# A state-space layer with a mixture of experts: blocks of the scan joined in pairs, and the residual written into PSUM

## What is computed

```python
xz = rms(xn) @ in_proj.T;  x_s, z = split(xz)            # 512 channels each
u = silu(conv4(x_s) + conv_b)                            # causal, 4 taps, per channel
dt_raw, B, C = split(u @ x_proj.T)                       # 16, 16, 16
delta = softplus(dt_raw @ dt_proj.T + dt_b)
h[t] = exp(delta[t] * A) * h[t-1] + (delta[t]*u[t]) * B[t]   # 16 states per channel
y[t] = sum_s h[t, :, s] * C[t, s] + u[t] * D
mamba = (y * silu(z)) @ out_proj.T + xn
ffn = top-2 of 8 experts, w2(silu(w1 xn) * (w3 xn)), weighted by the gate
```

## Time and profile before

| | before |
|---|---|
| median of three runs | 2660.86 us |
| profiled execution: its own time / its span | 2653.93 / 2652.2 us |
| TensorE busy | 2292.8 us, 86% |
| VectorE busy | 2459.2 us, 93% |
| ScalarE busy | 1658.9 us, 63% |
| GpSimd busy | 2031.0 us, 77% |
| mean granted TensorE clock | 0.936 |

### The profile page before, as it was taken

The page is one execution under the profiler, slowest core; times in us unless marked ns, Lnnn a source line. Parts: engine busy times, 40 slices in busy tenths (PEclk is TensorE's granted clock), DMA queues, the critical chain, the costliest instruction groups (busy, mean ns, idle before and its releaser), DMA issues. The chain is left out here.

```text
span 2652.2 us, 47132 instructions
## 1 busy us (share of the span) xinstructions
PE 2292.8 (86%) x14442; PEld 1986.7 (75%) x14442; DVE 2459.2 (93%) x4041; ACT 1658.9 (63%) x4137; POOL 2031.0 (77%) x1607
## 2 busy tenths in 40 slices
PE   3958789899999999998999989999989899998665
PEld 2855578878787887877888877888877787887554
DVE  7679999999999999999999999999999999999997
ACT  3940566666666666666666666666666666666653
POOL 3430678888888888888888888888888888888883
PEclk7858899999999999999999999999999999999776
DMA  7216045565555555555555555555555555542451
GB/s 244 92 40 216 29 124 156 154 176 152 161 151 152 157 160 171 158 157 153 155 160 155 166 163 151 158 156 160 154 162 164 156 152 157 159 113 52 96 100 32
DMA packets 267099, 379.38 MB, mean 143 GB/s; under 512 B 21492, under 2 KB 158324, under 8 KB 266852
## 3 DMA queue, kind: packets, MB, share of 16 engines
q1 hardware_dynamic: 236196, 332.26, 40.2%
q0 software_dynamic: 28480, 43.94, 10.1%
q10 hardware_dynamic: 2176, 0.18, 0.1%
HBM read 332.59 MB, written 52.10 MB: 145 GB/s over the span
## 5 line engine op out<-in xcount | busy, mean ns | idle before, releaser
L475 POOL TENSOR_TENSOR h<-du,bbc 128x512 f32<-128x512 f32 x1024 | 1362.5, 1354 | 505.3 <-PE HT L1305 375.3
L1071 DVE TENSOR_TENSOR_SCAN h<-DA,carry,h 128x256 f32<-128x256 f32 x2048 | 1417.7, 734 | 91.4 <-ACT DA L748 79.0
L748 ACT ACTIVATE DA<-delta,alog 128x256 f32<-128x256 f32 x2048 | 882.6, 468 | 212.2 <-DVE h L1071 200.9
L1305 PE MATMUL HT<-ident,h 128*128 128x128 f32 x4096 | 665.8, 288 | 260.5 <-DVE yT L1082 259.1
L1305 PEld LDWEIGHTS HT<-ident,h 128*128 128x128 f32 x4096 | 496.6, 148 | 416.2 <-issue 375.2
L1082 DVE SCALAR_TENSOR_TENSOR yT<-HT,cT,yT 128x512 f32<-128x512 f32 x960 | 698.5, 728 | 3.1 <-PE HT L1305 3.1
L1354 PE MATMUL G<-xtT,W 128*128 128x128 f32 x2160 | 273.2, 281 | 0.0
L1368 PE MATMUL G<-W,fill 128*128 128x256 f32 x1080 | 271.8, 397 | 0.0
L1361 PE MATMUL G<-xtT,W 128*128 128x128 f32 x2160 | 263.4, 275 | 0.0
L1354 PEld LDWEIGHTS G<-xtT,W 128*128 128x128 f32 x2160 | 261.1, 198 | 0.0
L1361 PEld LDWEIGHTS G<-xtT,W 128*128 128x128 f32 x2160 | 252.2, 192 | 0.0
(11 more groups left out here) (183 smaller groups left out, 2986.6 us busy)
## 6 DMA issues: line engine op xcount, KB each, us to landing
W<-in_w_T_dram SPq DMA_DIRECT2D x405, 512.0 KB, 4.2
bbc<-b_dram SPq DMA_DIRECT2D x256, 256.0 KB, 4.3
xraw<-in_x_dram SPq DMA_DIRECT2D x64, 256.0 KB, 2.7
xn_dram<-W SPq DMA_DIRECT2D x8, 1032.0 KB, 14.0
W<-in_x_dram SPq DMA_DIRECT2D x32, 256.0 KB, 6.7
moe_dram<-fill SPq DMA_DIRECT2D x32, 256.0 KB, 4.0
out_dram<-tmpA SPq DMA_DIRECT2D x32, 256.0 KB, 2.2
out_dram<-moe_dram POOLq DMA_DIRECT2D x32, 256.0 KB, 4.4
```

The lines of the kernel that those rows point to most:

```text
L475: pool.tensor_tensor(h[:, v % RING], du[:, b, 2 * q:2 * q + 2, :], bbc[:, s // 2 % BRING, s % 2, :].unsqueeze(1).to_broadcast([P, 2, T]), ...
L748: i = act.activation(DA[:, v % 2, k, :], delta[:, b, c, :], ACT.Exp, scale=nega[:, c, s:s + 1])
L1071: i = dve.tensor_tensor_scan(h[:, v % RING, k, :], DA[:, v % 2, k, :], h[:, v % RING, k, :], carry[:, b, s, c:c + 1], ALU.mult, ALU.add)
L1305: i = pe.transpose(HT[:, k, c * P:(c + 1) * P], h[:, (2 * s + c // 2) % RING, c % 2, k * P:(k + 1) * P], ident[:, :])
```

## The change

Blocks 2 to 29 are joined in pairs of the same batch row, 512 time steps in all (`LONG = 2` short blocks stay at either end). The number of units stays: a unit of a pair is one chunk (k = 0 to 3) of one state over 512 steps, still 128x512 elements. So `scan` and `make_da` are one instruction of 128x512 instead of two of 128x256, `keep_carry` comes once per four units, and TensorE turns a state's four units once all four are scanned: unit u at step u + 4, added at step u + 6. The ring `h` has three groups of four units in pairs (eight units before), `delta`, `du`, `u2` hold two pairs each, as rows of 512 of which a front writes one half of 256. The front of block n is done in block n - 2 instead of n - 1, and its back in block n + 2 instead of n + 1 (other places for the first and last blocks). Weight slots go from 5 to 3 experts, the ring of B rows from 4 to 3.

The residual is written by ScalarE into PSUM `FA` at step 26 (before: into SBUF at step 17); the output product starts on it (`start=False`) at steps 27 and 28, and ScalarE copies the sum into `res` at step 30. VectorE's add `result` is gone.

```diff
-            def make_da(blk, v):
-                (j, b), (s, q) = blk, divmod(v, 2)
...
-                for k in range(2):
-                    c = 2 * q + k
-                    i = act.activation(DA[:, v % 2, k, :], delta[:, b, c, :], ACT.Exp, scale=nega[:, c, s:s + 1])
...
+                if is_long(n):
+                    i = act.activation(DA[:, g % 2, :], delta_pair[n // 2 % 2][:, k, :], ACT.Exp, scale=nega[:, k, s:s + 1])
...
+                if is_long(n):
+                    i = dve.tensor_tensor_scan(h(g), DA[:, g % 2, :], h(g), carry[:, b, s, k:k + 1], ALU.mult, ALU.add)
...
+                if is_long(n):
+                    pool.tensor_tensor(h(g), du_pair[n // 2 % 2][:, k, :], bbc[:, g // 4 % BRING, :], ALU.mult).then_inc(s_dbu, 1)
...
+                if k == 0:
+                    pe.wait_ge(s_scan, g + (4 if is_long(n) else 2))
...
+            def residual(n):
+
+                act.wait_ge(s_xres, 16 * (n + 1))
+                if n + 5 <= NB:
+                    act.wait_ge(s_sp, 2 * (n + 5))
+                act.wait_ge(s_y, 2 * n + 2)
...
+                    act.activation(FA[:, t, :], xraw[:, t, :], ACT.Identity, bias=at_col(nm, q),
...
+            def result(n):
+                act.wait_ge(s_omm, NT * (n + 1))
+                wait(act, s_mamba, 16 * n)
+                act.wait_ge(s_delta, min(n + 5, NB))
+                act.copy(res, FA[:, :, :]).then_inc(s_res, 1)
...
-                                  start=(c == 0), stop=(c == CH - 1))
+                                  start=False, stop=(c == CH - 1), skip_group_check=True)
```

More of the change, by code:

```diff
@@ L208, in build @@
         NPAR = 16 * 6
[L210 to L230, removed]
@@ new lines, in turned, with tile_start, tiles_at, fills @@
+        def turned(g, after=0):
+            return [u for u in range(max(0, g - after - 8), min(g - after + 1, UNITS)) if turn_at[u] + after == g]
+        def tile_start(i):
+            return 2 * U * (J0 + i // PER) + U * (i % PER // len(XT_UNITS)) + XT_UNITS[i % len(XT_UNITS)]
+        def tiles_at(g, stage):
+            for i in range(NTILES):
+                if tile_start(i) + stage == g:
+                    return i
+            return None
+        def fills(i, ring):
+            return i // ring + 1
@@ L278, in build @@
[L278 to L284 removed]
+        BACK = {"z0": -1, "tanh_z0": 0, "silu_z0": 1, "z1": 2, "tanh_z1": 3, "silu_z1": 4, "y0": 4, "gate_y0": 6, "y1": 5,
+                "gate_y1": 7, "reload": 7, "oacc": 26, "out0": 27, "out1": 28, "result": 30}
+        AT = {(name, n): U * max(n - 2, 0) + at for name, at in FRONT.items() for n in range(1, NB)}
@@ L424, in _ @@
+            for g in range(UNITS):
+                step(g)
+            store_out(NB - 1)
+            sp.wait_ge(s_bst, 16 * NB)
+            sp.wait_ge(s_mamba, 16 * NB)
+            sp.wait_ge(s_add, 16 * NB)
         @block.gpsimd
@@ L569, in _ @@
+            for g in range(UNITS):
+                step(g)
+            add_result(NB - 1)
         @block.scalar
@@ L857, in _ @@
+            for g in range(UNITS):
+                step(g)
+            residual(NB - 1)
+            result(NB - 1)
         @block.vector
@@ L1177, in _, with step @@
-            run(step)
-            last = (JB - 1, 1)
-            for u in range(32 - LAG, 32):
-                add_state(last, u)
+            def step(g):
+                scan(g)
+                tile_a2(g)
+                for u in turned(g, 2):
+                    if state_of(u)[0]:
+                        add_state(u)
+                tile_ha(g)
+                if g == ROUTE:
+                    route()
+                    place()
+                    invert()
+                for q in range(2):
+                    for n in due(f"silu_z{q}", g):
+                        silu_z(n, q)
+                    for n in due(f"gate_y{q}", g):
+                        gate_y(n, q)
+                for q in range(2):
+                    for n in due(f"silu_u{q}", g):
+                        silu_u(n, q)
+                for q in range(2):
+                    for n in due(f"sp{q}", g):
+                        relu_ln(n, q)
@@ L1181, in _, with transpose_x @@
+            for g in range(UNITS):
+                step(g)
+            for g in range(UNITS, UNITS + 4):
+                for u in turned(g, 2):
+                    add_state(u)
             for q in range(2):
-                silu_z(*last, q)
-            for q in range(2):
-                gate_y(*last, q)
-            result(*last)
+                gate_y(NB - 1, q)
         @block.tensor
         def _(pe):
-            def transpose_x(j, b):
-                n = number(j, b)
+            def transpose_x(n):
@@ L1447, in _ @@
+            for g in range(UNITS):
+                step(g)
+            for g in range(UNITS, UNITS + 4):
+                for u in turned(g):
+                    transpose_h(u)
+            for q in range(2):
+                y_mm(NB - 1, q)
             for t in range(NT):
-                out_mm(*last, t)
+                out_mm(NB - 1, t)
 def kernel(**inputs):
```

1005 lines of the change are left out of this document (494 added, 511 removed), and 2 rows, old and new, of the table SLOTS.

## The result

The changed kernel takes 2639.1 us, median of 9 runs (2632.3 to 2645.8), against 2660.9 (9 runs of the kernel before beside them). The ratio is 0.9915, 95% interval 0.9892 to 0.9937, so it is 0.85% faster. The profiled execution has a span of 2636.2 us; before it was 2652.2, so the two traces differ by 16.0 us.

What follows compares the result with a forecast made beforehand. The prediction took a loop of GpSimd's leg, VectorE's handover and TensorE's leg as the bound, not VectorE alone. From 2653.93 us profiled, -56 for blocks and +19 for clock falls gave 2617 us, range 2575 to 2652.

Steps and rivals of the forecast that it cites:

- Scan and decay: VectorE's scan of 512 near 1.27 us, saving 0.12 a unit; ScalarE's decay near 0.68, saving 0.2 us on GpSimd's path.
- The two legs: GpSimd's stretch, VectorE's handover and TensorE's stretch form the block's loop: 24.2, 2.06 and 48.8 us, together 75.1; chance 0.50.
- Today the loss falls where GpSimd is awaited anyway: Kernel before, step 23: TensorE's half-clock loss of 1.7 us was said to fall where GpSimd is awaited.
- TensorE's leg: From TensorE's turning to the end of the next H1: 50.49 us falls by 1.7 to 48.8 as waits for VectorE shrink.
- Turning behind it waits 0.5 + 1.6 = 2.1 us.: At step 32 VectorE arrives 1.7 us early, the GpSimd term does not, so TensorE's turning waits 2.1 us.
- The clock, +19 us: TensorE falls to half clock after its new wait in four blocks of ten, 1.7 us each, over 28 blocks.
- Ends: I put them at nothing, within 8 us.: Short blocks, the crowded front of block 2 and the tail were together taken to change nothing, within 8 us.
- VectorE alone: Rival: VectorE sets the pace, so all 4.4 us a block come through, 124 us, giving 2530 us; chance 0.12.
- Clock in every block: Rival: TensorE's clock falls in every block, taking back 48 of the 56 us, giving 2646 us; chance 0.17.
- GpSimd's operations longer: Rival: large operations and driving terms lengthen GpSimd's path by 3.5 us a block, +42 us, giving 2696 us; chance 0.10.
- Front and back two blocks away: Rival: doing front and back two blocks away causes an unseen wait of 1 us a block, 2645 us; chance 0.11.
- Residual and copy at nothing: ScalarE's residual and copy, steps 26 to 30, put at nothing; if uncovered, 1.2 + 0.6 us a block.

Runs made afterwards that it cites:

- before_wait_after: Kernel before, without pairs, with GpSimd's wait for the exponential moved behind the driving term of step 27: 2672.5 us, ratio 1.0027 to 1.0063.
- ring_end: Changed kernel with the last two short blocks using all three groups of state slots in turn, not two: 2634.7 us.
- wm_vector: Changed kernel with the front's exp minus 1 moved from GpSimd to VectorE at its step 23: 2610.2 us.
- pairs_only: Changed kernel with the residual as before: ScalarE makes it in SBUF, VectorE adds it, ScalarE's copy is gone: 2640.9 us.
- split_scan: Changed kernel with each 128x512 scan of VectorE cut into two of 128x256, the state's link between halves left out: 2646.6 us.
- wm_later: Changed kernel with exp minus 1, correction and delta of GpSimd's front each one step later, du still at 27: 2737.2 us.

## Why the prediction was right, and what was wrong in it

2617 us was forecast, in a range of 2575 to 2652, with 0.76 for faster; 2639 came, and 2638.0 in the profiled run, from which the sum was made. The sign and the loop of two legs held, the size was 22 us off. Step by step:

- *Scan and decay.* 1.276 us and 0.685 for 1.27 and 0.68; a plain unit is 1.83 us, 0.12 shorter, and VectorE gave up 3.9 us a block (busy 69.6 for 73.5 from block 4 to 28, against "near 69"). Right.
- *The two legs.* In the block shown, GpSimd 24.08 for 24.2, handover 2.07 for 2.06. Right, and the experiments show that both legs bind: a block is 1.0 us shorter for a scan 0.96 earlier on the one, 1.14 for 1.4 to 1.7 on the other, against 0.25 for 3.8 on VectorE. In the means GpSimd's leg gained 0.56 us and not 0.2, since 24.36 was not the mean before: "Today the loss falls where GpSimd is awaited anyway" fails for five of 24 blocks, in which the fall hit H1 and the leg took 25.6 us.
- *TensorE's leg.* 49.39 for 48.8 in the block shown, and 49.72 in the mean. "Shrink by the 20 x 0.12 us that VectorE gains there" was to close all 1.7 us of its waits; the mean of the waits in this leg went from 1.68 only to 0.94 us, of which 0.79 is still for VectorE's adds and 0.15 for the gather. The leg gained 0.57 us and not 1.7. This term was mis-sized by a factor of three: 1.15 us came off a block, where 2.0 was the sum, and the blocks gave 36 us and not 56.
- *"Turning behind it waits 0.5 + 1.6 = 2.1 us."* Wrong by half: VectorE's wait of 1.52 (mean 1.42) came as foretold, but TensorE waited 1.09 (mean 0.91). It reached that turning 0.7 us earlier against the scan of step 32, not 1.6.
- *The clock, +19 us.* Wrong with it: a window over the second stretch was granted 1.00 in 23 of the 24 blocks and 0.97 in one, and there the fall stood behind another wait, for a gather (TensorE):

```profile
1855.47 0.44 PE L1403 MATMUL G<-ident,W 128*128 128x128 f32 x2 [2.06 <-DMA W<-xn_dram,token]
...
1856.38 3.38 PE L1282 MATMUL FB<-xrT,inT 128*128 128x256 f32 x8
```

  That block took 77.15 us. The price of a fall was about right: 1.5 us in before_wait_after, for 1.7.
- *"Ends: I put them at nothing, within 8 us."* This is the step that left the error in the total: +6.75 and +13.08 us. That the ring of the short blocks has two groups and that of the pairs three, and that they meet at one step, could be read in the code beforehand. ring_end shows 4 us of it, and 7 us beside wm_vector. Another 2.7 us is the residual ahead of the last output product, by the comparison with pairs_only. The other 6 at the end and the 6.75 at the start (2.3 in ring_end's trace) lie under waits for ScalarE's decays and tanh of z in the rows above; no run tried them, so their cause is open.
- The terms for blocks and clock were off in opposite senses (-36 for -56, 0 for +19), so that their sum, -36 for -37, hides it. That the two cancel was luck.
- *Rivals.* VectorE alone: out by split_scan. Clock in every block: out, but it is what turned before_wait_after. GpSimd's operations longer: out, they took 3.65, 2.37, 2.37 and 2.92. Its argument was a misreading, though. "The place of operands alone can cost 0.54" took L499 for slower than L494 by its operands. L573, the same operation now, takes 2.34 to 2.38 us in the first four blocks, which have no expert tiles, and 2.91 to 2.97 in the next 27; in wm_later it takes 2.36 or less in every block, and L569 takes the 2.9 us. In either case the long one is the first large operation behind the gather and scatter of a tile: it is the place in the queue, and its cause is open. Front and back two blocks away: a wait of 1 us a block does not show. The only new wait of TensorE is the one for the gather, 0.3 us a block.
- *Residual and copy at nothing*: within 2 us from both sides in the time, but 2.7 us at the end that the sum did not have.

## What to carry to other kernels

Before you count what a faster engine saves, find the loop that closes from block to block and write down which engine holds each piece of it; test it by giving the "busy" engine its old load back, which cost 7.5 us here, and by moving one operation to it from an engine with a lower share, which gained 29. Read the legs as means over many blocks: the one block that the prediction was built on hid five of 24 that were 1.2 us longer. An instruction's price in a queue is its length plus the wait that it carries: a driving term cost 1.25 us, or 3 us more where it opened a state. Where two regimes of a ring meet, go through the few steps by hand; in these two traces the ends took back more than half of what the blocks gave.

## What was not expected of the hardware

The same edit changed sign with the kernel it was put in (-27 us beside the pairs, +11 without them), and the sign came with the clock: without falls the edit would have gained the kernel before some 8 us (an estimate, 28 blocks of 0.3), but TensorE's clock fell behind the second of two waits of about 2 us in 18 of 24 blocks, where it had done so in five. A fall costs 1.3 us on H1 (3.29 for 1.95) and 1.4 on the eight matmuls of the experts' last product (3.27 for 1.89), and only its place in the loop decides whether the block gets 1.5 us longer. The waits at the head of TensorE's leg, 0.5 to 1.5 us in blocks 4 to 27 except block 21, had no fall behind them; the waits of 3.34 and 3.44 us shown above had one, and so had the 2.06 us of block 21 and the 1.93 us ahead of the last output product.
